# One attention-plus-experts block on one core: row norms moved from VectorE to ScalarE, ones written by a transfer, and a few items of the written-out order moved by a step

## The reference, cut to what matters

```python
h = _layernorm(x, axis=-1) * (1 + ca) + sa            # layernorm: (x - mean) / sqrt(var + 1e-5)
x = x + ga * attention(h, ...)                        # 16 heads, causal, rotary part, rms norm of kv
h = _layernorm(x, axis=-1) * (1 + cb) + sb
x = x + gb * experts(h, ...)                          # 8 heads x 16 experts, top 2, gelu
```

## Time and profile before

| | us |
|---|---|
| median of 3 runs | 3006.73 |
| lowest and highest | 3003.34, 3007.7 |
| the profiled execution, its own time | 3005.16 |
| span of the profiled execution, first to last instruction | 3003.4 |
| TensorE busy in the span | 2831.3 (94%) |
| VectorE, ScalarE, GpSimd busy | 1885.4, 1807.1, 1314.8 |
| mean granted TensorE clock, share of full speed | 0.986 |

### The profile page before, as it was taken

One profiled execution on the slowest core, in us unless ns is written; L12 is line 12 of the kernel. 1 busy time (PEld: TensorE's weight loads), 2 busy tenths in 40 slices (PEclk: granted clock), 3 DMA queues, 4 the chain that ended last, 5 costly groups with the idle time before them and its releaser, 6 DMA issues.

```text
span 3003.4 us, 51558 instructions
## 1 busy us (share of the span) xinstructions
PE 2831.3 (94%) x16460; PEld 1257.2 (42%) x16460; DVE 1885.4 (63%) x4634; ACT 1807.1 (60%) x2148; POOL 1314.8 (44%) x1356
## 2 busy tenths in 40 slices
PE   6789999999999999999999999999999999999999
PEld 2234444444444444444444444444444444444433
DVE  5475756657667566676666665666656657566553
ACT  1245665566755667556674566655766566655686
POOL 4312555135552364524644246442465235552354
PEclk8699999999999999999999999999999999999999
DMA  6202453034430444204442044320453124431343
GB/s 142 45 24 58 114 129 83 26 89 109 120 89 2 103 109 127 68 2 123 109 107 68 17 126 118 95 54 26 129 129 87 38 61 113 125 85 26 74 124 91
DMA packets 176245, 252.54 MB, mean 84 GB/s; under 512 B 50797, under 2 KB 82557, under 8 KB 175885
## 3 DMA queue, kind: packets, MB, share of 16 engines
q1 hardware_dynamic: 168988, 247.26, 32.3%
q10 hardware_dynamic: 6996, 1.99, 0.3%
HBM read 159.13 MB, written 12.63 MB: 57 GB/s over the span
## 4 chain that ended last, share of the span: by engine, by line
PE 84%; DVE 7%; issue 3%; ACT 1%; SPq 1%; DMA 0%; POOL 0%; POOLq 0%; DVEq 0%; ACTq 0%
PE ps L1230 17%; PE ps L1267 17%; PE ps L1285 16%; PE ps L1251 8%; PE ps L417 8%; PE ps L463 4%; PE ps L465 2%; PE ps L504 2%; PE ps L515 2%; PE ps L534 2%; DVE front L631 1%; PE ps L491 1%; DVE rest L1387 1%; DVE front L560 1%; PE ps L522 1%
## 5 line engine op out<-in xcount | busy, mean ns | idle before, releaser
L1351 ACT ACTIVATE rest<-ps 128x1024 f32<-128x1024 f32 x1024 | 993.9, 1024 | 355.2 <-PE ps L1267 355.1
L1333 ACT ACTIVATE rest<-ps 128x1024 f32<-128x1024 f32 (+3 forms) x768 | 608.8, 810 | 562.3 <-PE ps L1230 549.0
L1440 POOL TENSOR_TENSOR rest<-rest 128x512 f32<-128x512 f32 x480 | 629.6, 1312 | 577.9 <-DVE rest L1387 568.1
L1387 DVE SCALAR_TENSOR_TENSOR rest<-ps,b2c,wide 128x512 f32<-128x512 f32 x512 | 383.7, 750 | 528.0 <-PE ps L1285 495.0
L1267 PE MATMUL ps<-wide,w1s 98*128 98x512 f32 x2048 | 643.2, 434 | 11.5 <-ACT rest L1351 8.7
L1285 PE MATMUL ps<-rest,w2s 128*32 128x512 f32 x4096 | 547.2, 606 | 0.6 <-ACT rest L1351 0.6
L557 DVE CUSTOM_DVE_ANT_0 rest<-ps,maskd 128x256 f32<-128x256 f32 (+3 forms) x1024 | 458.6, 486 | 137.5 <-PE ps L417 129.7
L1430 POOL TENSOR_SCALAR_AFFINE_SELECT rest<-rest 128x256 f32<-128x256 f32 x512 | 204.4, 407 | 749.7 <-ACT rest L1333 746.8
L1230 PE MATMUL ps<-wide 49*128 49x512 f32 (+3 forms) x2304 | 483.8, 510 | 7.5 <-ACT rest L1333 5.6
L1267 PEld LDWEIGHTS ps<-wide,w1s 98*128 98x128 f32 x2048 | 346.3, 189 | 236.4 <-ACT rest L1351 103.2
L560 DVE TENSOR_REDUCE front<-ps 128x1 f32<-128x512 f32 x512 | 328.7, 683 | 88.5 <-PE ps L417 84.5
(11 more groups left out here) (137 smaller groups left out, 2320.7 us busy)
## 6 DMA issues: line engine op xcount, KB each, us to landing
wide<-gate_rows SPq DMA_DIRECT2D x1024, 128.0 KB, 2.8
wide<-front SPq DMA_DIRECT2D x480, 64.0 KB, 2.0
wide<-front SPq DMA_DIRECT2D x192, 128.0 KB, 2.3
ao<-in_x SPq DMA_DIRECT2D x16, 512.0 KB, 4.9
heads<-front SPq DMA_DIRECT2D x64, 128.0 KB, 2.4
xs<-in_x SPq DMA_DIRECT2D x16, 512.0 KB, 5.0
out<-xs SPq DMA_DIRECT2D x16, 512.0 KB, 3.3
wide<-ao SPq DMA_DIRECT2D x96, 64.0 KB, 2.3
```

Of the source, the lines that this page charges most:

```text
L1333: nc.scalar.activation(L.pt[:, u % PTS, :, f:HALF], L.ps[:, 2 * (u % 2):2 * (u % 2) + 2, 0:HALF - f], ACT.Exp, scale=SCALE).then_inc(S["c_ ...
L1351: nc.scalar.activation(L.hm[:, u % HM, :], bank(2 * (u % 2), 2), ACT.Gelu).then_inc(S["e_gelu"], 1)
L1387: v.scalar_tensor_tensor(out=dst, in0=bank(L2 + q % 2), scalar=L.b2c[:, e:e + 1], in1=L.gb[:, q // 2 % GB, q % 2, :], op0=ALU.add, op1=ALU ...
L1440: g.tensor_tensor(dst, dst, L.gy[:, k % GY, :], ALU.add).then_inc(S["e_add"], 1)
```

## The change: what it does

`norm_rows` and the "xn" item go to ScalarE: an activation Identity with a per-row scale (rstd) and a per-row bias (-mean * rstd). VectorE forms the biases in one small instruction, and ScalarE waits for that. In the opening `norm_rows` now stands on ScalarE behind the late transfers. For the next image it stands behind the gelus of steps 10 and 11 instead of on VectorE in steps 11 and 12. The two rows of ones are written by a transfer of SyncE from a small tile of ones, and `front_ones` is left to the opening. Some items of the expert stage stand one step later, two items of step 25 change places, two "row" items move to the last step, and one "pair" item moves from the last step of an image to slot 19 of the next.

```diff
+def norm_bias(v, L):
+    v.wait_ge(L.S["e_nr"], 1)
+    v.scalar_tensor_tensor(out=L.nbias[:, :], in0=L.mv[:, :, 0], scalar=-1.0, in1=L.rstd[:, :], op0=ALU.mult,
+                           op1=ALU.mult).then_inc(L.S["e_nb"], 1)
-def norm_rows(v, L, c):
-    v.wait_ge(S["e_nr"], 1)
+def norm_rows(act, nc, L, c):
+    act.wait_ge(S["e_nb"], 1)
     for t in range(4 * c, 4 * c + 4):
-        v.tensor_scalar(L.ao[:, t, :], L.ao[:, t, :], L.mv[:, t, 0:1], L.rstd[:, t:t + 1],
-                        ALU.subtract, ALU.mult).then_inc(S["e_nn"], 1)
+        nc.scalar.activation(L.ao[:, t, :], L.ao[:, t, :], ACT.Identity, bias=L.nbias[:, t:t + 1],
+                             scale=L.rstd[:, t:t + 1]).then_inc(S["e_nn"], 1)
# item "xn", on VectorE: only the bias; on ScalarE: wait for it, then four tiles
-        for t in range(4):
-            v.tensor_scalar(L.xn2[:, t, :], L.xs[:, 4 * c + t, :], L.tmv[:, t, 0:1], L.tstd[:, t:t + 1], ALU.subtract,
-                            ALU.mult).then_inc(S[f"d{c}_xn"], 1)
+        v.scalar_tensor_tensor(out=L.tbias[:, :], in0=L.tmv[:, :, 0], scalar=-1.0, in1=L.tstd[:, :], op0=ALU.mult,
+                               op1=ALU.mult).then_inc(S[f"d{c}_nm"], 1)
+    elif kind == "xn":
+        act.wait_ge(S[f"d{c}_nm"], 1)
+        for t in range(4):
+            nc.scalar.activation(L.xn2[:, t, :], L.xs[:, 4 * c + t, :], ACT.Identity, bias=L.tbias[:, t:t + 1],
+                                 scale=L.tstd[:, t:t + 1]).then_inc(S[f"d{c}_xn"], 1)
# ones of the inputs
-def input_ones(g, L, c):
-    g.memset(L.x2[3 * FD:XS, c, :, :].bitcast(F32), 1.0).then_inc(L.S[f"d{c}_one"], 1)
+def input_ones(sp, L, c):
+    sp.dma_start(L.x2[3 * FD:XS, c, :, :].bitcast(F32).rearrange("r h (a p) -> r (h a) p", p=P),
+                 L.ones[:, :].unsqueeze(1).broadcast_to([2, FH * HALF // P, P])).then_inc(L.S[f"d{c}_one"], 16)
# opening: ScalarE behind its transfers, VectorE only the bias
+            norm_rows(act, nc, e, 0)
+            norm_rows(act, nc, e, 1)
-            norm_rows(v, e, 0)
-            norm_rows(v, e, 1)
+            norm_bias(v, e)
-AHEAD = 3
+AHEAD = 2
-PLACES += [..., (19, 0), (20, 0), ...]
+PLACES += [..., (19, 0), (19, 1), (20, 0), ...]
-    at(10, ("tm", 1, 0))
-    at(11, ("tm", 1, 1), ("tlo", 1, 0))
-    at(12, ("tlo", 1, 1), ("lg", 1), ("chain", 1, 1), ("chain", 1, 2))
-    at(14, ("exp", 1))
+    at(11, ("tm", 1, 0))
+    at(12, ("tm", 1, 1), ("tlo", 1, 0))
+    at(13, ("tlo", 1, 1), ("lg", 1), ("chain", 1, 1), ("chain", 1, 2))
+    at(15, ("exp", 1))
     for k in range(3, 18):
-        at(13 + (k - 3) // 2, ("chain", 1, k))
-    at(21, ("gt", 1))
+        at(14 + (k - 3) // 2, ("chain", 1, k))
+    at(22, ("gt", 1))
-    at(25, ("rope", 4), ("kc", 1))
+    at(25, ("kc", 1), ("rope", 4))
-    at(54, ("row", 0, 1))
-    at(61, ("row", 1, 0))
+    at(63, ("row", 0, 1), ("row", 1, 0))
# step loop: ScalarE
+                    if q in (10, 11) and img + 1 < B:
+                        norm_rows(act, nc, L, q - 10)
# step loop: VectorE
-                    if q in (11, 12) and img + 1 < B:
-                        norm_rows(v, L, q - 11)
+                    if q == 10 and img + 1 < B:
+                        norm_bias(v, L)
# GpSimd: input_ones in slots 33 and 41 and front_ones in step 1 are gone
# SyncE: input_ones(sp, L, 0) ahead of move_inputs of the first half; input_ones(sp, L, 1) behind move_gates(0)
-                        if more:
-                            front_row(sp, L, R, 0, 1)
                 if more:
                     front_row(sp, L, R, 1, 0)
+                    front_row(sp, L, R, 0, 1)
```

More of the change, by code:

```diff
@@ L106, in build @@
         L.neg1 = sb("neg1", [1, P])
+        L.ones = sb("ones", [2, P])
         L.gkv = sb("gkv", [P, 1])
@@ L130, in build @@
         L.rstd = sb("rstd", [P, NT])
+        L.nbias = sb("nbias", [P, NT])
         L.kvar = sb("kvar", [P, NT])
@@ L137, in build @@
         L.tstd = sb("tstd", [P, 4])
+        L.tbias = sb("tbias", [P, 4])
         L.ao = sb("ao", [P, NT, C])
@@ L162, in build @@
         L.s_pa = sem("s_pa")
-        routing = ["st", "ad", "rs", "xn", "hi", "lo", "r", "e", "x2", "gd", "one"]
+        routing = ["nm", "st", "ad", "rs", "xn", "hi", "lo", "r", "e", "x2", "gd", "one"]
         L.names_a = ["a_x", "a_mod", "p_rt", "p_sh", "p_add", "p_ng", "p_c2", "p_c3", "p_mq2", "p_mk2", "p_mq3", "p_mk3", "c_s", "c_exp",
@@ L167, in build @@
         L.names_b = ["e_l1", "e_gelu", "e_l2", "e_gb0", "e_gb1", "e_gb2", "e_gb3", "e_gy", "e_add", "e_xb", "e_nx", "e_nm",
-                     "e_nst", "e_nr", "e_nn", "f_p", "f_v", "f_a", "f_sq", "f_sh", "f_rt", "f_add", "f_ks", "f_mf", "f_mq0", "f_mk0", "f_mq1",
+                     "e_nst", "e_nr", "e_nb", "e_nn", "f_p", "f_v", "f_a", "f_sq", "f_sh", "f_rt", "f_add", "f_ks", "f_mf", "f_mq0", "f_mk0", "f_mq1",
                      "f_mk1", "f_cq", "f_ck", "f_cc", "f_ng", "f_row00", "f_row01", "f_row10", "f_one"] \
@@ L669, in item_scalar @@
         nc.scalar.activation(L.ec, L.ec, ACT.Exp).then_inc(S[f"d{c}_e"], 1)
+    elif kind == "xn":
+        c = item[1]
+        act.wait_ge(S[f"d{c}_nm"], 1)
+        for t in range(4):
+            nc.scalar.activation(L.xn2[:, t, :], L.xs[:, 4 * c + t, :], ACT.Identity, bias=L.tbias[:, t:t + 1],
+                                 scale=L.tstd[:, t:t + 1]).then_inc(S[f"d{c}_xn"], 1)
     elif kind == "tr":
@@ L916, in opening @@
     ] + [(e.b2c[FD * k:FD * k + FD, :], e.b2.rearrange("e o -> o e")) for k in range(4)]
-    consts = 5 + NE + 2
+    consts = 6 + NE + 2
     with nc.Block() as block:
@@ L963, in _ @@
             g.memset(e.neg1[:, :], -1.0).then_inc(e.s_c, 1)
+            g.memset(e.ones[:, :], 1.0).then_inc(e.s_c, 1)
             for k in range(NE):
@@ L1243, in values @@
                     pe.wait_ge(S["e_gy"], NQ - 1)
-                    pe.wait_ge(S["f_one"], 2)
                     RE[img - 1].wait(pe, L, ("v", 1))
@@ L1258, in inner @@
                     pe.wait_ge(S[f"d{c}_x2"], 16 * 24)
-                    pe.wait_ge(S[f"d{c}_one"], 1)
+                    pe.wait_ge(S[f"d{c}_one"], 16)
                 if u >= 2:
@@ L1468, in _ @@
                         g.tensor_tensor(L.xs[:, 0:4, :], L.xs[:, 0:4, :], bog, ALU.add).then_inc(S["e_xb"], 1)
-                    if q == 1 and img + 1 < B:
-                        g.wait_ge(S["c_pv"], NM)
-                        front_ones(g, L)
                     for item in eslots[img][q]:
@@ L1541, in _ @@
                 sp.wait_ge(S["c_s"], 2 * 32)
+                input_ones(sp, L, 0)
                 for j in range(CH):
@@ L1544, in _ @@
                 move_gates(sp, L, RA[img], 0)
+                sp.wait_ge(S["c_s"], 2 * 40)
+                input_ones(sp, L, 1)
                 sp.wait_ge(S["c_s"], 2 * NM)
```

13 lines of the change are left out of this document (1 added, 12 removed).

## The result

The changed kernel takes 3039.6 us (median of 4 runs, 3037.45 to 3044.76) against 3007.22 for the kernel before, run beside it: a ratio of 1.0112, 95% interval 1.0095 to 1.013. It is slower by 32 us, where +14 was forecast. The profiled execution took 3037.45, its span is 3035.7, against 3003.4 before, and TensorE's mean granted clock is 0.978 instead of 0.986.

What follows compares the result with a forecast made beforehand. TensorE bounds the kernel, busy 348.82 of 362.70 us an image. Terms +31.5, -8.4, -13.2, -7.1, +4.9, +2.4 and +4.2 sum to +14.3 on 3005.16: 3019.5, or 3021 as median; range 2985 to 3045.

Steps and rivals of the forecast that it cites:

- the rival of the cheap rows: Four norm rows on ScalarE take 1.2 us instead of 2.05, giving 3002 us; chance 0.13.
- The rival in which ScalarE absorbs B and C: Of the expert-stage stalls only step 7's 2.4 us is paid, giving 2982 (2963 without that too); chance 0.20.
- B: Step 12: TensorE waits for gelu 22, queued behind the next image's first norm rows and their bias; +2.6 us.
- C: Step 12: second "ht" waits for ScalarE's late read of the second tm; +2.0 us, then 0.4 to 0.9 before "qct".
- A: Step 7: xn rows on ScalarE delay gelu 16, so TensorE idles; +2.4 us in every image.
- the held bias: Rival: GpSimd instructions delay VectorE's bias, up to 0.9 us in step 7 and 1.3 in step 12; +16, 3037; 0.22 with clock.
- Step 25: "kc" ahead of "rope 4" removes most of the kc wait: -1.2 us an image, -8.4 in all.
- slot 19: The second pair item there costs TensorE 0.7 us idle in seven images, +4.9 in all.
- the opening: norm_rows behind ScalarE's transfers delays "kvt" and the chain after it by +4.2 us, unless transfers set the end.
- steps 7 to 14: Expert stage: stalls of 7.4 to 8 us against 3.4 removed; +4.5 taken in seven images, +31.5 in all.
- the lower clock: Rival: TensorE's granted clock drops behind stalls in steps 7 and 12, 14 x 0.95 = +13, 3034; 0.22 with held bias.
- tm has moved to step 11: -0.75: Step 10: TensorE's wait for VectorE's late read of "tr2" goes, -0.75 us an image.

Runs made afterwards that it cites:

- experiment 6: Changed kernel plus three unread TensorE matmuls in each of the waits before steps 9 and 12, keeping TensorE busy there: 3030.1 us, ratio 1.0080.
- experiment 15: Kernel before with only the ones written by transfer and the values' ones left to the opening: 2999.8 us, ratio 0.9987.
- experiment 1: Changed kernel with all row norms (opening, next image, xn) back on VectorE, everything else as changed: 2963.8 us, ratio 0.9855.
- experiment 11: Changed kernel with only the opening's eight rows back on VectorE: 3040.0 us, ratio 1.0117.
- experiment 12: Changed kernel with the items of steps 10 to 21 back in the steps of the kernel before: 3023.0 us, ratio 1.0059.

## Why the prediction was right or wrong

**Right: the row.** Forecast 0.59 and 2.05 for four. Measured 0.589 and 2.07 to 2.08, in both places:

```profile
L683 ACT ACTIVATE front<-xs,tbias,tstd 128x256 f32<-128x256 f32 x64 | 33.2, 589 | 22.3 <-DVE tbias L640 22.3
L336 ACT ACTIVATE ao<-ao,nbias,rstd 128x256 f32<-128x256 f32 x64 | 33.1, 588 | 47.4 <-DVE nbias L328 25.2 <-issue 22.1
```

That ends the rival of the cheap rows. The rival in which ScalarE absorbs B and C fell too: its condition, a bias ready by the end of gelu 21, was missed by 3.1 (bias at 1427.6, end of the gelus of step 10 at 1424.5).

**Right: the places and the size of the stalls at full clock.** A to C were forecast as 7.4 to 8 an image. With the clock kept (experiment 6) steps 0 to 15 are 61.13 - 53.06 = 8.1 longer than with the rows on VectorE. That sum is partly luck, as said below under the held bias.

**Right in kind: what goes.** Slot 35 -0.9 (experiment 15: 0.8), both waits behind the row copies, the wait of step 10, and of steps 12 to 14 those of 1.7 and 0.6; the 0.3 behind the copy stayed. Step 25 kept a wait of 0.67 where 0.3 was forecast, and slot 19 has one of 0.62 for 0.7. Order and ones together were forecast at -(3.4 + 1.2 + 1.9) x 7 - 7.1 + 4.9 = -47.7; experiment 1 gives -42.6.

**Right by the trace, open in its effect: the opening.** "kvt" moved from 28.22 to 33.57 and the opening grew by 5.4, forecast 4.2. ScalarE's transfers ended 0.9 later in this trace (26.5, not 25.6), which is most of the difference. The sign "a wait of the opening's first ht of some 4 us more" was wrong: it grew by 9.8, from 9.3 to 19.1, and kvt's own wait fell from 6.0 to 1.0, since the modulation had landed before VectorE came to its reads. The first image's attention was 5.5 shorter in the same trace, and experiment 11 can't tell whether that is a gift of the clock.

**Wrong: steps 7 to 14, forecast at +4.5 an image, and the last image at +2.4.** This is the step that failed, "steps 7 to 14, 7 x 4.5 = +31.5". Measured is +6.4 an image (the stage's 3.73, plus the 1.9 of the row copies and 0.8 of step 25 that went) and +5.2. These are 13.5 + 2.8 of the 18 us that the sum lacks (another 2.6 are the 0.37 that step 25 kept beyond the forecast in seven images). The mechanism, stalls behind ScalarE's rows, was right and the term was mis-sized, because the forecast took every matmul behind a stall at full speed and put the lower clock among the rivals. A to C with all that follows them cost 62.80 - 53.06 = 9.7 an image instead of 7.4 to 8. With TensorE kept busy in the waits the clock stayed, and 1.67 of that and 2.6 in the last image went. The lower clock stood among the rivals as 14 x 0.95 = +13, "3034" (by its own list of stalls, eight of A and seven of B, it is 15). The runs make its net 14 by the stages and 9.5 by the medians. The sum of that rival held, but not its working, which was luck: the clock does not fall behind every stall, a fall costs more than 0.95, two falls in one image do not add, and of the 3.1 gross an image nearly half comes back since B and C shrink by it.

**The other rival that came true is the held bias**, forecast at +16 on top. The bias takes 0.97 and 1.23 instead of 0.2. Taking the hold away within VectorE gives 12 back, taking the bias out of VectorE's queue as well gives 25. It didn't come on top of the sum, because other parts of the sum were too large. With the clock kept (experiment 6) C is 1.50 where 2.0 was forecast, and the 0.4 to 0.9 before "qct" did not come. Nor is A as large as forecast: without the 0.8 of the hold it would be some 2.0 instead of 2.4, an estimate from that trace. B without its hold is 2.5, as forecast. With a bias on GpSimd and the clock kept, steps 0 to 15 cost 58.75 - 53.06 = 5.7 more, not 7.9. So two errors of some 2 us an image cancelled, by luck, and the clock was left.

**A step that held in the sum and not by itself** is "tm has moved to step 11: -0.75". I credited the move and charged stalls B and C to the norms. With the norms on ScalarE the move is what makes most of B and C; undone, the kernel is 17 us faster (experiment 12). The prediction never asked what the changed order would cost if only the norms moved with it.

**Without cost, as forecast**: the transfers of the ones and GpSimd's freed time. SyncE's rotary transfers start 19.0 behind the expert stage's end after, 15.8 before, and TensorE's waits for a transfer out of `front` after the first image are small: 0.4 once before, 0.9 and 0.3 after.

The sign and the range (2985 to 3045) held. The 0.65 for slower was fair; the 0.22 for clock and held bias was too low, as both had a row of the trace that showed them at work.
